# A mask written into PSUM by ScalarE, a value projection placed earlier, and a reordered ending in a six-layer decoder kernel

## What is computed

```python
def local_attention(q, k, v):            # 16 heads of 64, windows of 32 tokens
    ...                                  # every window sees itself and the window before it
    mask = (it < jb) | (it > jb + w) | (jb == -1)
    sim = jnp.einsum('bhwie,bhwje->bhwij', bq, bk2) * QK_SCALE
    sim = jnp.where(mask, -jnp.finfo(sim.dtype).max, sim)
    attn = jax.nn.softmax(sim, -1)
    out = jnp.einsum('bhwij,bhwje->bhwie', attn, bv2)
for i in range(DEPTH):                   # DEPTH = 6
    x = attn_layer(shift_tokens(x), Wqkv[i], q_scale[i], k_scale[i], Wo[i]) + x
    x = ffn_layer(shift_tokens(x), ln_g[i], ln_b[i], W1[i], b1[i], W2[i], b2[i]) + x
```

## Time and profile before

| what | us |
|---|---|
| median of 3 runs | 2069.38 (2057.55 to 2073.07) |
| profiled execution, device time | 2072.66 |
| its span, first to last instruction | 2070.8 |
| time around the span | 1.9 |

### The profile page before, as it was taken

How to read it: one execution, slowest core, us unless ns; L and a number is a source line. 1 busy time by engine, 2 the same in 40 slices (tenths; PEclk the granted TensorE clock), 3 DMA queues, 4 the chain that set the end, 5 groups by cost and what they waited for, 6 DMA issues and landing times.

```text
span 2070.8 us, 47295 instructions
## 1 busy us (share of the span) xinstructions
PE 1946.3 (94%) x19198; PEld 1175.1 (57%) x19198; DVE 1516.5 (73%) x1744; ACT 1312.1 (63%) x1870; POOL 1012.5 (49%) x727
## 2 busy tenths in 40 slices
PE   6787888799999999999999999999999999999996
PEld 3121135366666666666666666666666666666665
DVE  4897446687778777877787777777787778777852
ACT  3387744476667666766676667666676667666755
POOL 6200123565556555655565655555555555555530
PEclk9799899899999999999999999999999999999997
DMA  3331010254333443334443435443444334443430
GB/s 120 45 77 26 12 39 6 80 136 104 101 100 101 124 122 101 94 100 128 125 103 98 108 101 137 110 107 92 108 128 129 90 91 111 113 111 83 114 95 14
DMA packets 106072, 195.91 MB, mean 95 GB/s; under 512 B 14432, under 2 KB 34912, under 8 KB 105600
## 3 DMA queue, kind: packets, MB, share of 16 engines
q1 hardware_dynamic: 105856, 192.88, 36.2%
HBM read 124.81 MB, written 54.79 MB: 87 GB/s over the span
## 4 chain that ended last, share of the span: by engine, by line
PE 78%; ACT 2%; issue 1%; POOL 1%; DVE 0%; ACTq 0%; POOLq 0%
PE ps L1414 16%; PE ps L1489 9%; PE ps L1444 9%; PE ps L1466 8%; PE ps L1500 8%; PE ps L1423 8%; PE ps L1521 6%; PE ps L1477 4%; PE ps L1454 4%; PE ps L1533 3%; PE ps L1439 2%; ACT l_v_tok L1586 1%; PE ps L1508 1%; POOL l_rot L1387 0%; ACT L1700 0%
## 5 line engine op out<-in xcount | busy, mean ns | idle before, releaser
L1387 POOL TENSOR_TENSOR l_rot<-l_rot,l_rot_s 128x1024 f32<-128x1024 f32 x192 | 455.2, 2371 | 1.0 <-DVE l_rot_s L1744 1.0
L1376 POOL COPY l_kb<-l_kb 128x512 f32<-128x512 f32 x95 | 63.1, 664 | 685.5 <-ACT l_kb L1620 685.5
L1390 POOL TENSOR_TENSOR l_rot<-l_rot,l_norms 128x1024 f32<-128x1024 f32 x192 | 365.2, 1902 | 15.0
L1732 DVE TENSOR_TENSOR l_rot<-ps,l_tab_c 128x1024 f32<-128x1024 f32 x192 | 234.9, 1224 | 165.5 <-ACT l_sq L1594 165.5
L1594 ACT ACTIVATE l_sq<-ps 128x1024 f32<-128x1024 f32 x192 | 196.8, 1025 | 206.5 <-PE ps L1414 204.0
L1744 DVE TENSOR_TENSOR l_rot_s<-ps,l_tab_s 128x512 f32<-128x512 f32 x384 | 245.5, 681 | 0.0
L1723 DVE TENSOR_REDUCE l_norms<-l_sq 128x16 f32<-128x1024 f32 x192 | 232.1, 1209 | 0.0
L1414 PE MATMUL ps<-l_wqkv,xsT 128*128 128x512 f32 x384 | 187.1, 611 | 16.9 <-ACT l_v_tok L1586 14.5
L1620 ACT ACTIVATE l_kb<-ps 64x1024 f32<-64x1024 f32 x192 | 195.7, 1019 | 1.1
L1466 PE MATMUL ps<-l_vb,l_pT 128*32 128x128 f32 x6144 | 188.0, 273 | 2.8 <-issue 1.4
L1603 ACT ACTIVATE l_norms<-l_norms 128x16 f32<-128x16 f32 x192 | 41.5, 216 | 233.1 <-POOL l_norms L1384 233.1
(11 more groups left out here) (171 smaller groups left out, 3198.1 us busy)
## 6 DMA issues: line engine op xcount, KB each, us to landing
l_vb<-v_scratch SPq DMA_DIRECT2D x336, 256.0 KB, 4.6
v_scratch<-l_v_tok SPq DMA_DIRECT2D x96, 512.0 KB, 4.9
l_vb<-v_scratch SPq DMA_DIRECT2D x48, 192.0 KB, 3.2
xsT<-xT SPq DMA_DIRECT2D x48, 135.8 KB, 2.5
l_xf<-xT SPq DMA_DIRECT2D x46, 128.0 KB, 2.3
stack<-scratch SPq DMA_DIRECT2D x72, 64.0 KB
l_wqkv_odd<-wqkv SPq DMA_DIRECT2D x9, 512.0 KB, 6.2
scratch<-parts SPq DMA_DIRECT2D x12, 256.0 KB, 2.6
```

The lines of the kernel that those rows point to most:

```text
L1387: nc.gpsimd.tensor_tensor(rot[:, t % 2, n], rot[:, t % 2, n], rot_s[:, n], ALU.add).then_inc(added, 1)
L1390: nc.gpsimd.tensor_tensor(rot[:, t % 2, n], rot[:, t % 2, n], norms[:, t % 2, n, :, None].broadcast_to([P, HEADS, DH]), ALU.mult).then_inc ...
L1732: nc.vector.tensor_tensor(rot[:, t % 2, 1 - r], slot(name, t).rearrange("p n (h d) -> p (n h) d", d=DH), tab_c[:, 1 - r, t % TILES, None, ...
```

## The change

It does six things.

1. The two mask matmuls go. `lay_mask(t - 1)` on ScalarE copies the mask (f32, in the constants, broadcast over the 16 heads, 128 x 1024) into the slot of the scores, behind the square of q(t) and ahead of the copy of the turned probabilities. `scores` waits for it (`mask_laid`).
2. All turns are issued as `matmul(..., is_transpose=True)` with `start` set only for the first of four in a bank.
3. `project_v(t)` moves from behind `values` to ahead of the mean and the scores; `copy_v(t)` on ScalarE moves ahead of the norm pieces and the second inverse norm.
4. The mean goes into slot 0, between the turned probabilities and the values. On VectorE the centring moves ahead of the sum of squares of q.
5. The loop ends at step 96 (`ENDING = ALL + 1`), and what is left is written out for PE, ScalarE and VectorE in an order of its own. The hidden chunks of a one-tile unit share one slot (`hidden_tile`, `gelu_tile`, `gate_tile`).
6. The constants are smaller (512 and 256 columns become 128), and the two casts on VectorE are gone.

```diff
         for t in range(ENDING):
+            if has(t):
+                plan(("v", t), 1)
             if b_norm is not None:
-                plan(("mean", b_norm), 1)
+                plan(("mean", b_norm), 0)
             if has(t - 1):
                 plan(("s", t - 1), 3)
             if has(t - 2):
                 plan(("o", t - 2), 0)
-            if has(t):
-                plan(("v", t), 1)
...
                 def scores(t):
                     wait_free(pe, "qT", t)
-                    wait_free(pe, "kT", t)
+                    wait(pe, mask_laid, t + 1)
...
-                    for n in range(2):
-                        rows = slice(64 * n, 64 * n + 64)
-                        nc.tensor.matmul(dst[:, n, :], mask_sel[rows, opening, :], mask[rows, :], start=True, stop=False,
-                                         skip_group_check=True)
...
+                def lay_mask(t):
+                    wait_free(act, "kT", t)
+                    nc.scalar.activation(slot("s", t).rearrange("p n (h k) -> p (n h) k", k=2 * WINDOW),
+                                         mask[:, int(t % TILES == 0), None, :].broadcast_to([P, HEADS, 2 * WINDOW]),
+                                         ACT.Copy).then_inc(mask_laid, 1)
...
                     if has(t):
                         square(t, 1)
+                    if has(t - 1):
+                        lay_mask(t - 1)
                     if has(t - 2):
                         copy_probs(t - 2)
                     if has(t):
                         inverse_norm(t, 0)
+                        copy_v(t)
...
                     if has(t):
                         cosine_part(t, 1)
+                    if b_norm is not None:
+                        centre(b_norm)
+                    if has(t):
                         sum_squares(t, 1)
...
+                turn_out(ALL - 2)
+                turn_probs(ALL - 1)
+                mean(WHOLE + 1)
+                values(ALL - 1)
+                project_out(WHOLE + 2)
+                turn_out(ALL - 1)
+                variance(WHOLE + 1)
+                hidden_tile(WHOLE)
+                project_out(WHOLE + 3)
+                project_ffn(WHOLE - 1)
+                mean(WHOLE + 2)
...
```

More of the change, by code:

```diff
@@ L1162, in layers @@
         WHOLE = LAYERS * BATCH - 1
+        ENDING = ALL + 1
         def span(u):
@@ L1196, in plan @@
             taken[n] += 1
-        for t in range(STEPS):
+        for t in range(ENDING):
             b_wo, b_norm, b_hid, b_y = pieces(t)
@@ L1544, in turn_back, with hidden_tile, mean, variance @@
                     m.then_inc(filled("x", u), 1)
-                for t in range(STEPS):
+                def hidden_tile(u):
+                    _, first, cols = span(u)
+                    pe.wait_ge(xg_ready, u + 1)
+                    take(pe, "h", u, 0)
+                    for c, (a, n) in enumerate(HC):
+                        for s in range(2):
+                            w = w1_sb[:, s * HIDDEN + a:s * HIDDEN + a + n]
+                            m = nc.tensor.matmul(slot("h", u, 0)[0:n, s, c * P:c * P + cols], w, xg[:, first:first + cols],
+                                                 start=True, stop=True)
+                    m.then_inc(filled("h", u, 0), 1)
+                def mean(u):
+                    moment("mean", xf_ready, 32 * (u + 1), u)
+                def variance(u):
+                    moment("var", fsquared, u + 1, u)
+                for t in range(ENDING):
                     b_wo, b_norm, b_hid, b_y = pieces(t)
@@ L1578, in _ @@
                         turn_back(b)
+                turn_out(ALL - 2)
[9 more added lines that the diff above has]
+                mean(WHOLE + 2)
+                variance(WHOLE + 2)
+                hidden_tile(WHOLE + 1)
+                mean(WHOLE + 3)
+                project_ffn(WHOLE)
+                variance(WHOLE + 3)
+                project_ffn(WHOLE + 1)
+                hidden_tile(WHOLE + 2)
+                turn_back(WHOLE - 1)
+                hidden_tile(WHOLE + 3)
+                project_ffn(WHOLE + 2)
+                turn_back(WHOLE)
+                project_ffn(WHOLE + 3)
+                turn_back(WHOLE + 1)
+                turn_back(WHOLE + 2)
+                turn_back(WHOLE + 3)
             @block.scalar
@@ new lines, in gate_tile @@
+                def gate_tile(u):
+                    _, first, cols = span(u)
+                    for c, (_, n) in enumerate(HC):
+                        dve.wait_ge(gelu_ready, len(HC) * u + c + 1)
+                        m = nc.vector.scalar_tensor_tensor(out=gel[0:n, c, first:first + cols],
+                                                           in0=slot("h", u, 0)[0:n, 0, c * P:c * P + cols],
+                                                           scalar=vec[0:n, V_B1 + c:V_B1 + c + 1],
+                                                           in1=gel[0:n, c, first:first + cols],
+                                                           op0=ALU.add, op1=ALU.mult)
+                    m.then_inc(emptied("h", u, 0), 1)
```

215 lines of the change are left out of this document (135 added, 80 removed).

## The result

The changed kernel takes 2073.94 us (median of 17 runs, 2069.89 to 2092.64) against 2064.28 for the kernel before (17 runs, 2057.55 to 2077.14). The ratio is 1.0049, with an interval of 1.0032 to 1.0067: no change by the 1% of the prediction, and yet a small loss that the runs do resolve. The execution that the profile shows took 2073.94, its span is 2072.1.

A forecast was written before the change was run, and what follows sets the result against it. The prediction took PE to bound the layers, busy for 67.81 of 68.24 us a unit. Its terms, 13 + 3 - 1.5 - 11.5 = +3 us, gave 2072.4 against the median, stated as 2073, with a range of 2042 to 2094.

The forecast's parts named there:

- The wo and y step: Layer steps where scores start once the mask is written: gains of 0.35 us (wo) and about 0.07 (y).
- The norm step: Layer step where the mean waits 0.98 us for the copy of the turned probabilities; the step loses 0.25.
- The hidden step: Layer step after the norm step: late centring delays the turned output by 1.12 us; step end 34.2, before 33.1.
- The first rival: In the layers the waits don't form, a unit gains 1.7 us, and the time is 2013; chance 0.22.
- The second: ScalarE's mask write outlasts a copy: every 0.1 us beyond 1.02 costs 9 us in all; chance 0.13.
- The third: The ending keeps its length, its waits being dependencies, so -11.5 us falls away: 2084; chance 0.13.
- A unit by 22: Four layer steps (norm, hidden, y, wo) taken as +0.6 us, over 22 units +13 us.
- Steps 95 and 96: Last two steps of the loop: variance 1.7 us later, mean and scores about 1.4; together +3 us.
- The ending: From the last whole hidden product to the end: 38.5 us rather than 50.0, so -11.5.
- the walk: Tracing the ending's 26 products in new order through their waits: 37 us, or 42 if the clock falls.
- The opening: Steps before the first feed-forward piece: k waits less for v, -1.5 us, between -10 and 0.
- The base: Starting time for the sum: profiled execution of the kernel before, 2072.66 us, 3.3 above the median of the runs.

The follow-up runs named there:

- e1: The changed kernel, but in norm steps alone ScalarE copies the turned probabilities ahead of the mask write; 2058.02 us, 0.9952 of the kernel before.
- e2: The changed kernel, but VectorE does the sum of squares ahead of the centring again; 2060.61 us, 0.9960 of the kernel before.
- e7: The changed kernel without any mask, so it computes something else and only prices the mask; 2042.35 us, 0.9874 of the kernel before.
- e3: The changed kernel with both the edits of e1 and e2; 2036.45 us, 0.9849 of the kernel before.
- e4: The changed kernel with the last units in the old loop's order, without the written-out ending; 2101.15 us, 1.0153 of the kernel before.
- e6: The changed kernel with the mask matmuls back on PE and no mask write on ScalarE; 2065.21 us, 0.9979 of the kernel before.
- e8: The kernel of e3 without any mask, so it only prices the mask there; 2015.21 us, 0.9747 of the kernel before.
- e9: The kernel of e3, but outside norm steps the mask write stands ahead of the square of q; 2055.11 us, 0.9938 of the kernel before.
- e10: The same kernel as e3, run again in more rounds; 2033.34 us, 0.9833 of the kernel before.
- e5: The kernel before with ScalarE's mask write, new turns and constants, but v, mean and ending as they were; 2193.31 us, 1.0608 of the kernel before.

## Why the prediction was right, and where it wasn't

**What bounds.** Right: in the layers PE was the bound, and what left it was replaced by waits for ACT and DVE.

**The wo and y step.** Predicted gains of 0.35 and 0.07, measured 0.30 and 0.11.

**The norm step.** Predicted a mean at 9.73 after a wait of 0.98 and a next k at 15.34; the trace has 9.74, 0.93 and 15.37. e1 takes the wait away and gets 0.94 back, so the cause is shown.

**The hidden step.** The chain mean, centring, sine part, difference, exponentials, Ln was predicted to start the turned output at 18.00, and it started at 18.09; the step was put at 34.2 - 15.34 = 18.86 and has 18.87. e2 shows that the sum of squares queued behind the centring is the cause. That the mask pair and a wait for the mask would cancel there is only nearly so: the pair is 0.32, and the wait is 0.20, as e7 shows with 18.67 without any mask. The turned output starts 0.09 later than predicted, and the two errors make up for each other, so the agreement to 0.01 is luck.

**The first rival** (no waits, 2013) was wrong about the changed kernel, and the two orders of e3 turn it into 66.5 + 0.5 = 67.0 a unit and 2033 to 2036. That ScalarE is busy for only 45 of 68 us was no argument: from the first square to the copy of the turned probabilities it works without a gap, and that copy is what the mean waits for. **The second** (a long mask write) is out: the write lasts 1.02 (mean 1.023 over 96), as its neighbours do. **The third** (an ending that keeps its length) is out by e4.

The Trainium skill, "ScalarE: Activation LUTs", in the note on where ScalarE writes, has PSUM faster than SBUF as the target. Here the write from SBUF to PSUM lasts 1.02, and the exponentials, of the same size from SBUF to SBUF, last 1.06 (means 1.023 and 1.058): less by 0.035 us, which agrees, though the function is another. To the next start it is 0.95 against 0.96, and that distance is what the queue pays. The neighbours that the prediction priced the write by read PSUM and write SBUF; they last 1.02 to 1.03 too, with 0.90 to 0.92 to the next start. So leaving the term out of the sum was right.

**The sizes that were off.**

- *A unit by 22.* I took +0.6 and got 13. The undisturbed unit has +0.71, so 15.6, and the rest to 19.9 is disturbed units: what the stretch has beyond 22 usual units is 6.3 in the kernel before and 10.6 in the changed one. My term was a typical unit by a count and missed these. Laid side by side, step by step, the surplus lies in three places. Steps 90 and 94, in which outputs of the last layer are turned back, have 3.2 (3.0 before). In five hidden steps, the first of a layer each, v ahead of the scores now waits 0.33 to 0.35 for VectorE's sine part of k, about 1.9 in all (none before); e6, e7 and e8 have this wait too, so it belongs to the new place of v. And ten times PE pauses inside the values, 5.1 by the starts (six times and 2.9 before):

```profile
1045.04 1.95 PE L1448 MATMUL ps<-l_kb,l_qT 128*32 128x128 f32 x64
1046.79 1.52 PE L1470 MATMUL ps<-l_vb,l_pT 128*32 128x128 f32 x48
1048.95 0.65 PE L1470 MATMUL ps<-l_vb,l_pT 128*32 128x128 f32 x16 [0.64 <-issue]
```

  The code of the values has waits only ahead of their first product, and the profile names nothing for the pause. Such pauses are missing in e6, e7 and e8, where ScalarE writes no mask, make 0.9 in e9, 5.0 to 6.9 in e1 to e4 and e10, and 10.2 in e5; but the kernel before has 2.9 of them without any write by ScalarE. What makes them stays open; the scores themselves don't wait longer in these units.
- *Steps 95 and 96.* +3 predicted, +6.5 measured. The variance of step 95 comes 1.7 later, as predicted. From the turned probabilities to the scores of step 96 it is 2.2 longer, where I had 1.4. The remaining 2.6 are TensorE's clock, a term that I had put at nothing. In the changed kernel the timeline of PE in step 96 reads:

```profile
2012.47 1.94 PE L1481 MATMUL ps<-cst,l_o_tok 128*128 128x128 f32 x8 [0.87 <-ACT l_rstd L1728]
2014.21 2.61 PE L1433 MATMUL ps<-cst,l_rot 128*128 128x128 f32 x16
2017.21 1.06 PE L1458 MATMUL ps<-cst,l_prob 128*128 128x128 f32 x8 [0.39 <-ACT l_qT L1634]
2021.25 0.46 PE L1512 MATMUL ps<-l_xf,cst 128*128 128x128 f32 x2 [2.98 <-ACT l_pT L1634]
2021.64 2.91 PE L1448 MATMUL ps<-l_kb,l_qT 128*32 128x128 f32 x64
2024.30 2.70 PE L1470 MATMUL ps<-l_vb,l_pT 128*32 128x128 f32 x64
```

  There is no v left to cover the copy, so 2.98 are idle. The scores last 2.91 and the values 2.70 where they take 1.96 and 1.93 in the layers, the turned output and the turned q and k 1.94 and 2.61 rather than 1.06 and 1.91. The windows from k(95) to the end of the last whole hidden product, the kernel before, the changed one and e3:

```profile
1984.35:2020.83 36.48, 32.79 (x391) 23.23 (x390) 20.05 (x25) 22.34 (x30) 9.49 (x7) 1.00 0.40 106
1992.75:2035.69 42.94, 35.45 (x386) 26.13 (x385) 20.05 (x25) 24.51 (x32) 9.53 (x7) 0.92 0.34 90
1968.19:2005.59 37.40, 32.31 (x387) 22.95 (x386) 19.99 (x25) 24.13 (x32) 9.49 (x7) 1.00 0.40 103
```

  The clock stayed at 1.00 before and fell in the changed kernel. With both orders changed (e3) it stayed at 1.00 again, and the stretch is 0.9 longer than before rather than 6.5; in e10, the same kernel, it is 38.5 at 0.96.
- *The ending.* -11.5 predicted, -13.6 measured. It took 36.4, where the walk gave 37 with a full clock and 42 with the old one. The clock was 1.00 in its first part and 0.77 in its second, between the two. By the walk's own two values a clock in between gives about 39 to 40, so the walk was some 3 us too long, and the 38.5 that I took was 2 too careful. The denser ending (PE busy for 25.7 of 36.4 us, before for 32.1 of 50.0) did keep more of its clock than the old one (0.97 and 0.57), as the Trainium skill, "TensorE: Matmul & The Clock Gate", Part 1, has it: activity releases the slower state.
- *The opening.* -1.5 predicted, -0.1 measured. PE's turned q and k wait for POOL's rotation there, 9.7 in 6 times. What k no longer waits for v it waits for POOL: the waits swapped their names.
- *The base.* The three runs of before that I had put its median at 2069.38. Over 17 it is 2064.28, 5.1 lower. The difference of the medians is +9.7 where I said +3.6, so the change was put 6.1 too low. In the traces the change is 12.8 where I had 3, and the four sizes above are that error (6.9 + 3.5 + 1.4 - 2.1 = 9.7); the interval of the medians, 6.6 to 13.8, has the 12.8 in it.

The predicted time, 2073.0, and the measured one, 2073.94, agree to 1 us by luck: the base was 5.1 too high and the change 6.1 too low, and the terms of the change were off by up to 7 us in both directions. What held is the mechanism, the two new waits and the shorter ending, each with its size in the timeline.

## What to carry to other kernels

An instruction moved to an engine with free time is paid for at the place where it is queued: ask which copy or sum now stands behind it, and who waits for that. In an in-order queue, put what frees a bank or has its input already ahead of what only has to be there later; here two such swaps turned a loss of 0.5% into a gain of 1.7%. And look at the units that aren't typical before multiplying a typical one by its count: here they held 4 of the 20 us.

## What the runs showed of the hardware

- ScalarE's write of 128 x 1024 from SBUF into PSUM lasts 1.02 us with the next start 0.95 behind, although its input is a mask in short runs of 64 elements read again and again; a copy from PSUM to SBUF of the same size has 1.02 and 0.90 (line 1634 to the next start, 1028.29 to 1029.19), the exponentials from SBUF to SBUF 1.06 and 0.96.
- In step 96 PE's clock fell toward the lower of its two levels (1.2 GHz of 2.4). The first sign is the turned output at 2012.47, which lasts 1.94 us rather than 1.06, behind waits of 1.30 and 0.87; over 2012.47 to 2017.21 the granted clock is 0.67. In the kernel before the waits at that place are 0.47 and 0.87, and the clock is 1.00. In the layers the changed kernel has gaps of 0.93 and 0.85 in each unit, and the granted clock stayed at 1.00.
- The first k of the layers starts at 358 to 376 us in profiles of kernels that share the code ahead of it: more than the difference that was to be measured. The granted clock over 240 to 300 us goes from 0.71 to 0.97 among them.
- PE can pause for 0.17 to 1.12 us in the middle of 64 products between which no wait stands, with nothing named by the profile.
